# Expert slots of a routed feed-forward block taken in twos on TensorE, with deeper rings of row and result buffers

## The reference

```python
x = x + conv(_ln_c(x), registers, qkv_w, qkv_b, out_w, out_b)   # neighbourhood attention, 12 heads of 16, 7 x 7 keys + 16 registers
t = _to_tokens(x)                                               # 4608 tokens x 192
t = t + ffn(_ln_t(t), gate_w, w1, w2, w3, sw1, sw2, sw3)

# ffn, with xf = the 4608 normalized tokens
scores = softmax(xf @ gate_w.T)                                 # 16 experts
topw, topi = top_k(scores, 2)
h = silu(einsum('td,eid->tei', xf, w1)) * einsum('td,eid->tei', xf, w3)     # 512 wide
y = einsum('tei,edi->td', h * comb[:, :, None], w2)             # comb: topw at topi, else 0
z = silu(xf @ sw1.T) * (xf @ sw3.T) @ sw2.T                     # shared expert, 1024 wide
return y + z
```

## Time and profile before

| | us |
|---|---|
| median of 3 runs | 1377.29 (1372.33 to 1387.77) |
| the profiled execution | 1377.1 |
| its span | 1375.5 |
| PE busy | 1202.9 (87%) |
| DVE busy | 646.2 (47%) |
| ACT busy | 557.9 (41%) |
| POOL busy | 507.0 (37%) |

### The profile page before, as it was taken

One profiled execution on the slowest core, in us unless ns is written; L12 is line 12 of the kernel. 1 busy time (PEld: TensorE's weight loads), 2 busy tenths in 40 slices (PEclk: granted clock), 3 DMA queues, 4 the chain that ended last, 5 costly groups with the idle time before them and its releaser, 6 DMA issues. The chain is left out here.

```text
span 1375.5 us, 32552 instructions
## 1 busy us (share of the span) xinstructions
PE 1202.9 (87%) x10666; PEld 957.1 (70%) x10666; DVE 646.2 (47%) x1439; ACT 557.9 (41%) x1569; POOL 507.0 (37%) x651
## 2 busy tenths in 40 slices
PE   5788469888889888886899999999999999999990
PEld 3455357666666666664576767679999999988880
DVE  2578658787888778875622222222222222222220
ACT  2466557777777777771111111112222222221110
POOL 1235223333333233320066650003555555444442
PEclk9899789999999999998999999999999999999995
DMA  4567988888888878841122241347888888877754
GB/s 91 123 172 177 187 175 151 147 153 153 151 146 152 148 144 143 150 89 48 29 55 57 69 117 58 99 135 181 226 216 228 216 230 213 223 208 198 192 132 117
DMA packets 202034, 202.84 MB, mean 147 GB/s; under 512 B 51260, under 2 KB 170940, under 8 KB 201756
## 3 DMA queue, kind: packets, MB, share of 16 engines
q1 hardware_dynamic: 175020, 167.39, 51.6%
q0 software_dynamic: 26928, 34.31, 13.2%
HBM read 160.54 MB, written 44.66 MB: 149 GB/s over the span
## 5 line engine op out<-in xcount | busy, mean ns | idle before, releaser
L665 POOL DMA_INDIRECT acc_dram<-ys,lists x87 | 138.4, 1591 | 296.3 <-DVE ys L1173 128.8
L744 ACT ACTIVATE probs<-ps,nmax 128x330 f32<-128x330 f32 x432 | 228.5, 539 | 4.9 <-DVE nmax L996 2.9
L996 DVE TENSOR_REDUCE nmax<-ps 128x2 f32<-128x660 f32 x216 | 181.3, 840 | 72.6 <-PE ps L1250 68.6
L1281 PE MATMUL ps<-ident_sb,probs 128*110 128x128 f32 x1296 | 187.8, 279 | 24.9 <-DVE probsT L935 24.1
L1166 DVE TENSOR_TENSOR m_h<-m_sg,ps 128x512 f32<-128x512 f32 x87 | 59.8, 687 | 301.1 <-ACT m_sg L796 297.8
L1281 PEld LDWEIGHTS ps<-ident_sb,probs 128*110 128x110 f32 x1296 | 149.6, 137 | 49.4 <-DVE probsT L935 36.9
L1448 PE MATMUL ps<-xa,w13r 128*128 128x128 f32 x1392 | 169.9, 276 | 0.3 <-ACT xa L790 0.3
L1448 PEld LDWEIGHTS ps<-xa,w13r 128*128 128x128 f32 x1392 | 162.3, 192 | 0.5 <-issue 0.5
L1367 PE MATMUL ps<-c_x,sw13a_sb 64*128 64x384 f32 x768 | 145.7, 491 | 9.1 <-DMA c_x<-xt_dram 4.6
L783 ACT ACTIVATE s_sg<-ps 128x384 f32<-128x384 f32 x96 | 47.1, 490 | 241.3 <-PE ps L1367 236.8
L736 ACT COPY probsT<-ps 110x384 f32<-110x384 f32 x216 | 103.4, 479 | 99.2 <-PE ps L1281 98.7
(11 more groups left out here) (124 smaller groups left out, 1660.0 us busy)
## 6 DMA issues: line engine op xcount, KB each, us to landing
w13r<-in_w13a SPq DMA_DIRECT2D x87, 512.0 KB
ksp<-k_dram SPq DMA_DIRECT2D x216, 115.5 KB
w13r<-in_w13b SPq DMA_DIRECT2D x87, 256.0 KB
qsp<-q_dram POOLq DMA_DIRECT2D x216, 48.0 KB, 3.7
k_dram<-a_ks SPq DMA_DIRECT2D x72, 99.0 KB, 3.8
ksp<-in_mask_k SPq DMA_DIRECT2D x36, 185.6 KB
w_sb<-in_w SPq DMA_DIRECT2D x8, 768.0 KB, 6.2
vst<-v_dram SPq DMA_DIRECT2D x72, 82.5 KB
```

What stands on the lines that cost most here:

```text
L665: nc.gpsimd.indirect_dma_start(acc_dram, bass.IndirectOffsetOnAxis(ap=lists[:, j, 0:1], axis=0), ys[:, j % V8, :], None, compute_op=ALU.ad ...
L744: ins = nc.scalar.activation(probs[:, p % 2, hh, :], ps[:, 2 * (p % 2) + hh, 0:KW], ACT.Exp, bias=nmax[:, p % 2, hh:hh + 1], accum_out=sum ...
L996: nc.vector.tensor_reduce(nmax[:, p % 2, :], ps[:, 2 * (p % 2):2 * (p % 2) + 2, 0:KW], AX.X, ALU.max, negate=True).then_inc(b_nm, 1)
L1281: ins = tr(ps[0:CH, 4 + hh, 128 * k:128 * (k + 1)], probs[:, p % 2, hh, CH * k:CH * (k + 1)], ident_sb[:, :])
```

## The change

The slots are taken in pairs (0, 1), (2, 3) and so on; slot 86 is alone. On PE, `up` is cut into `up_rows` (the full-row products) and `up_tails` (the half-row products). A pair goes: transposes of the two slots of the next pair, full-row products of both slots, half-row products of both, then `y_mm` of both slots of the pair before. ACT and DVE follow that order. `V8` goes from 8 to 12 and `AHEAD` from 7 to 11 (gathered rows and results), `RING` from 4 to 6 (weights), and `xa` and `m_h` from two buffers to four. `add_rows`, `gather` and `load_w13` are unchanged but for these numbers.

```diff
-    V8, AHEAD = 8, 7
+    V8, AHEAD = 12, 11
     USED = (2 * T - EX) // 128 + EX
-    RING = 4
+    RING = 6
...
-        xa = place("xa", [128, 2, XW], f32, at)
+        xa = place("xa", [128, 4, XW], f32, at)
...
-        m_h = place("m_h", [128, 2, INTER], f32, at)
+        m_h = place("m_h", [128, 4, INTER], f32, at)
...
-                if j >= 2:
-                    act.wait_ge(d_a, j - 1)
-                    act.wait_ge(d_b, j - 1)
-                nc.scalar.copy(xa[:, j % 2, :], ps[:, 4 + j % 2, 0:XW]).then_inc(d_xTev, 1)
+                if j >= 4:
+                    act.wait_ge(d_a, j - 3)
+                    act.wait_ge(d_b, j - 3)
+                nc.scalar.copy(xa[:, j % 4, :], ps[:, 4 + j % 2, 0:XW]).then_inc(d_xTev, 1)
...
-            for j in range(USED):
-                if j + 1 < USED:
-                    xT_out(j + 1)
-                d_silus(j)
+            xT_out(1)
+            for j in range(0, USED, 2):
+                for v in range(j + 2, min(j + 4, USED)):
+                    xT_out(v)
+                for v in range(j, min(j + 2, USED)):
+                    d_silus(v)
...
-            for j in range(USED):
-                h_out(j)
+            for j in range(0, USED, 2):
+                for v in range(j, min(j + 2, USED)):
+                    h_out(v)
                 if j:
+                    y_out(j - 2)
                     y_out(j - 1)
             y_out(USED - 1)
...
-            def up(j):
+            def up_rows(j):
...
+            def up_tails(j):
+                g = 2 * (j % 2)
                 for f in range(4):
                     for k, made in enumerate((d_a, d_b)):
...
             x_T(0)
-            for j in range(USED):
-                if j + 1 < USED:
-                    x_T(j + 1)
-                up(j)
+            x_T(1)
+            for j in range(0, USED, 2):
+                pair = range(j, min(j + 2, USED))
+                for v in range(j + 2, min(j + 4, USED)):
+                    x_T(v)
+                for v in pair:
+                    up_rows(v)
+                for v in pair:
+                    up_tails(v)
                 if j == 0:
                     pe.wait_ge(d_down, 16 * EX // 2)
                     pe.wait_ge(c_z, 3 * NB)
                 else:
+                    y_mm(j - 2)
                     y_mm(j - 1)
             y_mm(USED - 1)
```

More of the change, by code:

```diff
@@ L1163, in h_out @@
                 dve.wait_ge(d_b, j + 1)
-                if j >= 2:
-                    dve.wait_ge(d_yps, j - 1)
-                nc.vector.tensor_tensor(m_h[:, j % 2, :], m_sg[:, j % 2, :], ps[:, 2 * (j % 2) + 1, :],
+                if j >= 4:
+                    dve.wait_ge(d_yps, j - 3)
+                nc.vector.tensor_tensor(m_h[:, j % 4, :], m_sg[:, j % 2, :], ps[:, 2 * (j % 2) + 1, :],
                                         ALU.mult).then_inc(d_h, 1)
@@ L1448, in up @@
                         mm(ps[:, g + k, 128 * f:128 * (f + 1)], w13r[:, j % RING, k, 128 * f:128 * (f + 1)],
-                           xa[:, j % 2, 0:128], start=f == 0, stop=False, skip_group_check=True)
+                           xa[:, j % 4, 0:128], start=f == 0, stop=False, skip_group_check=True)
+            def up_tails(j):
+                g = 2 * (j % 2)
                 for f in range(4):
@@ L1453, in up @@
                         ins = mm(ps[:, g + k, 128 * f:128 * (f + 1)], w13r[half, j % RING, 2, 128 * f:128 * (f + 1)],
-                                 xa[half, j % 2, 128:256], start=False, stop=True, skip_group_check=True)
+                                 xa[half, j % 4, 128:256], start=False, stop=True, skip_group_check=True)
                         if f == 3:
@@ L1463, in y_mm @@
                 for k in range(4):
-                    ins = mm(ps[:, 6 + j % 2, 0:D], m_h[:, j % 2, 128 * k:128 * (k + 1)],
+                    ins = mm(ps[:, 6 + j % 2, 0:D], m_h[:, j % 4, 128 * k:128 * (k + 1)],
                              w2_sb[:].rearrange("p e k d -> p (e k d)")[:, ds(e * (4 * D) + k * D, D)],
```

## The result

The changed kernel took 1472.42 us (median of 4 runs, 1468.14 to 1485.03), the kernel before 1382.53 beside it (median of 4, 1372.33 to 1404.75). The ratio is 1.069, with a 95% interval of 1.057 to 1.081: the change makes the kernel 6.9% slower. (An execution more than 1.5% above the fastest of its kernel, here the 1404.75, counts as slow and is left out of every ratio.) I had forecast 1388.5, 0.8% slower, and a range of 1362 to 1403. The sign was right; the time lies far outside the range. The profiled execution took 1468.15 us, and its span is 1466.4, where it was 1375.5.

A forecast was written before the change was run, and what follows sets the result against it. The serial chain of adds was taken as the bound: 945.4 + 75 x 5.03 + 11 x 4.31 + 3.5 (last landing) + 13.3 (output) = 1386.9, plus 1.6 gives 1388.5 us, 0.8% slower; range 1362 to 1403.

The forecast's parts named there:

- the main step: Chain of adds in stage D: mean step beside weight loads 5.03 us; wrong if below 4.7 or above 5.2.
- What bounds the kernel: Stage D to the end: the serial chain of 87 adds on POOL, each awaiting the previous landing, sets the end, not PE.
- The saving on PE: PE in stage D: two mode changes a pair instead of four save 0.41 us a pair, 17.6 us; direct worth zero.
- The first add: Start of stage D's chain: the order in pairs delays it 5.8 us, from 939.59 to 945.4.
- I cost the loads at nothing: Two extra weight loads on SP, ahead of the last stage C stores: no cost; at worst 3.4 us uncovered.
- The gathers hold PE: PE in stage D: held by gathers once adds lag results by 13.4 us, at slot 20 to 25.
- The step of the chain: Adds beside weight loads: one clean step of 4.4 us and one met step of 5.63, taken as 5.03 in the mean.
- 75 x 5.03: Term of the sum: 75 chain steps with weight loads beside them, at 5.03 us each.
- The rule on queues: DMA engines: a met add pays for a packet, not the burst, so longer bursts would not raise the 5.63 us.
- Held and out of phase: Rival, chance 0.20: chain holds PE from slot 25, bursts meet each even slot's add; step 5.30, 1408.7 us.
- In phase: Rival, chance 0.14: adds settle in the gaps between loads; step 4.60, time 1356.2 us.
- PE's saving reaches the end: Rival, chance 0.06: the chain is not the bound, so 17.6 us less, 1359.5 us.

The follow-up runs named there:

- two chains: Adds of odd slots sent to a second tensor, merging left out: on the kernel before 1366.87 us (1.002), on the changed kernel 1356.87 us (0.993).
- its repetition: The changed kernel run once more, unaltered: 1467.25 us in one execution.
- the late gate: Changed kernel, load j held until a small POOL copy behind add j - 8 has run: 1382.11 us, 1.012; same idea on the kernel before: 1362.06 us, 0.999.
- both versions of two chains with pairs: Changed kernel with odd slots' adds in a second tensor: without merging the tensors 1356.87 us (0.993), with merging, complete, 1362.02 us (0.996).
- in pairs with the loads apart: Changed kernel, odd slot's load also waits for the full-row products of the next pair's first slot: 1428.75 us, ratio 1.045.
- the early gate: Each load also waits until an earlier add has been issued: changed kernel (add j - 8) 1522.97 us, 1.116; kernel before (add j - 6) 1487.24 us, 1.088.
- without loads: Changed kernel without the weight loads of slots 6 to 86: 1349.89 us, 0.988; kernel before without those of slots 4 to 86: 1355.8 us, 0.991.

## Why the prediction was right in sign and wrong in size

The sign is worth little: I gave 0.43 to no change and 0.37 to slower. By the sign of being wrong that I had named, a mean step above 5.2, the main step failed: it is 5.96.

**What bounds the kernel.** Right. The chain of adds set the end before and sets it after. The output copy waits for the last landing in both, and the steps behind the last load are the same 4.3 us.

**The saving on PE.** Right in place and in size. Pairs that run free start 8.79 us apart (957.62 to 966.41), where I had 8.77: 0.39 us saved a pair, or 0.2 for each change between full and half rows. On the end it was worth nothing, as said. In two chains it shows: from first add to last 43 pairs save 16.8 of the 22 us between 392.1 and 370.2, and most of the rest is the first add, which comes later in pairs while the last does not.

**The first add.** I had 945.4, and it was 957.4. The 5.8 us for the order in pairs measured 6.3. The other 11.4 us, in stage C, I did not foresee; what I wrote of it, "I cost the loads at nothing", is not what failed: the first weight load of stage D is issued at 923.59, long behind what waits. A row of the changed kernel shows a wait of PE there, a product of the shared expert that waits for its rows:

```profile
830.96 1.01 PE L1371 MATMUL ps<-c_x,sw13a_sb 64*128 64x384 f32 x2 [7.20 <-remote]
```

The kernel before has no such wait in stage C. It is there in this kernel and its repetition (7.2 and 6.5 us), and in the late gate and both versions of two chains with pairs (5.3 to 6.8), and absent with eleven gathers on the order of before, and in pairs with the loads apart, with the early gate and without loads; with seven gathers there is none above 1.9 us. In time it stands beside the data of the first eleven gathers. What causes it was not settled, and no run was made for it alone. The other 4 of the 11.4 us may be no more than what executions differ by: in the kernels without this wait and without a further copy in stage C, the first transposes start at 929.5 to 933.7. Some 11 of the 91 us therefore stay without a shown cause.

**The gathers hold PE.** Right: 19 waits of 3.8 us in the mean and 6.0 at most, the first at slot 17, where I had slot 20 to 25. I didn't say that they would pull the granted clock down to 0.90, but as adds lag their results by 9 us and more, this costs nothing on the path.

**The step of the chain: the step that failed.** My words were: "I take one clean step, 4.4, and one met step, the middle of 5.15 and 6.10, 5.63." The first half held. 34 of the 75 landings beside loads are clean (under 4.0 us, steps of 4.46 in the mean), 41 are met, so it is about one of each. The price of a met step did not hold. The mean landing of a met add is 6.3 us and its step 7.2, up to 9.04. In the kernel before the 30 met adds, by the same bound, have steps of 5.6, so my 5.63 was a right price for the old loads. The term "75 x 5.03" became 74 x 5.96 = 441, 64 us more; together with 12 us of the first add and 4 us for one more step behind the last load, that is, within half a microsecond, the 79.5 between my 1386.9 and the span of 1466.4. Bounding the step from above by 5.30 was the error in the range: that number came from a stretch with one load at a time, and the change doubled the burst. I held the price of a met add fixed while the thing it meets grew. The experiment with loads in twos on the kernel before shows this term alone: a step of 5.88 and a span 75 us longer, with PE's order and the first add as before. How much of a met step's price is the length of the burst and how much its phase is told apart only by the table above: two loads cost 2.2 to 2.5 us more where the first is 1 to 2 us ahead of the add, and 0.2 more where both come behind its start.

**The rule on queues.** I had cited the Trainium skill, DMA: Bandwidth & Descriptors, Queues, rings and completion order, for engines that take their queues in turn, a packet from each, so that a longer burst would not raise the price. The runs differ: an add 1 us behind a load landed in 4.7 us in the mean beside one load and in 7.0 beside two, and in the changed kernel the queue of the adds moved nothing for 2.5 us while that of the loads was 92% of the engines. The measurement decides. Once its data flow, the add does share the engines about evenly (33.6 and 30.2%), as the rule has it; it is the wait until then that was longer. Whether what is late there is the descriptors of the add or their fetching, no view shows.

**The rivals.** "Held and out of phase" was the nearest, with PE held and the burst on the adds, but not in place or price: 23 of 37 odd adds beside loads are met and 18 of 38 even ones, and the mean step is 1.5 us over a clean one (5.96 less 4.46), where it had 0.9. "In phase" did not come. "PE's saving reaches the end" was wrong for this kernel, and came true in part when the chain was cut in two (1366.87 to 1356.87).

## What to carry to other kernels

A serial chain of small indirect DMAs pays for what lies beside it on the same engines, and the price of a meeting depends on its phase and, where the burst starts first, on the length of the burst. Before an order of work is changed for the sake of one engine, ask which loads it releases together, and give the chain's step a price for that burst, not for the one that the old trace shows. If the loads have slack, send them out at a fixed point of the chain, and measure where: here 2 us made the difference between 8.8% slower and no loss.

## What the runs showed of the hardware that I had not expected

- A semaphore increment that stands behind an indirect DMA on POOL is seen by SP 0.6 us behind that instruction's start, while its own busy time is 1.6 us; put behind a small copy, the same signal comes at 2.6 us. As a clock for other queues the two are different points.
- An indirect add beside 1.5 MB of loads lands in up to 8.2 us, beside 0.75 MB in up to 5.9 (7.0 and 7.7 in the two kernels where nearly every add was made to meet one), beside gathers alone in up to 5.5, and with nothing beside it, at the end of the changed kernel, in 3.4 to 3.6.
- Two fewer changes between full-row and half-row products in a pair saved 0.39 us of PE (9.18 to 8.79).
- PE waited up to 7.2 us in stage C in some of the kernels with eleven gathers and an order in pairs, which no edit here explains.
